# Sums of gathered rows moved from TensorE to GpSimd, gathers spread evenly, and the selection's beats redrawn

## The reference, cut to what matters

```python
scores, idx = top_k(sim, 16)                       # two sides of 64 sub-keys, 8 heads
score = scores[0][..., :, None] + scores[1][..., None, :]
final_scores, pk_idx = top_k(score, 16)            # 16 of 4096 rows for every token and head
w = softmax(final_scores)
k = einsum('bnhk,bnhkd->bnhd', w, keys_table[ind])
v = einsum('bnhk,bnhkd->bnhd', w, values_table[ind])
```

## Time and profile before

| | |
|---|---|
| median of 3 runs | 13968.45 us (13955.31 to 13971.13) |
| the profiled execution | 13932.0 us, span 13929.9 us |
| TensorE (PE) busy | 12687.6 us, 91% |
| VectorE (DVE) busy | 10456.8 us, 75% |
| ScalarE (ACT) busy | 10198.2 us, 73% |
| GpSimd (POOL) busy | 5190.5 us, 37% |
| mean granted TensorE clock | 0.983 of full speed |

### The profile page before, as it was taken

How to read it: one execution, slowest core, us unless ns; L and a number is a source line. 1 busy time by engine, 2 the same in 40 slices (tenths; PEclk the granted TensorE clock), 3 DMA queues, 4 the chain that set the end, 5 groups by cost and what they waited for, 6 DMA issues and landing times.

```text
span 13929.9 us, 337634 instructions
## 1 busy us (share of the span) xinstructions
PE 12687.6 (91%) x87840; PEld 9681.5 (70%) x87840; DVE 10456.8 (75%) x37953; ACT 10198.2 (73%) x24147; POOL 5190.5 (37%) x4136
## 2 busy tenths in 40 slices
PE   6999999999999999999999999999999999999998
PEld 4776766767677667676676766767767677676776
DVE  7777777777777777777777777778777777777774
ACT  5777777777777777777777777777777777777776
POOL 3333333333333333333333333333333333333342
PEclk9999999999999999999999999999999999999998
DMA  2222222222222222222222222222222222222222
GB/s 72 81 79 80 83 79 82 79 81 81 80 80 81 82 81 79 80 84 78 81 81 80 83 79 78 82 81 82 79 80 83 79 81 81 81 81 79 80 84 60
DMA packets 612306, 1112.58 MB, mean 80 GB/s; under 512 B 134096, under 2 KB 150992, under 8 KB 610384
## 3 DMA queue, kind: packets, MB, share of 16 engines
q1 hardware_dynamic: 461648, 816.40, 19.6%
q0 software_dynamic: 131072, 268.70, 7.7%
q10 hardware_dynamic: 17696, 4.46, 0.1%
HBM read 1084.90 MB, written 4.19 MB: 78 GB/s over the span
## 4 chain that ended last, share of the span: by engine, by line
PE 54%; DVE 19%; ACT 11%; DVEq 8%; issue 7%; ACTq 0%; POOL 0%; POOLq 0%
PE p_d L1409 20%; PE p_g L1450 6%; PE p_s L1397 5%; PE p_s L1398 5%; ACT ew L1132 5%; DVE ew L907 5%; PE p_g L1360 3%; DVEq L645 3%; ACT prob L1221 2%; DVE rank_hot L888 2%; PE p_f L1344 2%; PE p_x L1562 2%; PE p_x L1499 2%; ACT gath L1175 1%; PE p_x L1555 1%
## 5 line engine op out<-in xcount | busy, mean ns | idle before, releaser
L1132 ACT ACTIVATE ew<-p_s 128x512 f32<-128x512 f32 x12288 | 7128.0, 611 | 2777.5 <-PE p_s L1398 2550.0
L627 POOL DMA_INDIRECT gath<-in_table,idx x4096 | 5166.5, 1261 | 8585.0 <-PE p_s L1398 8148.6
L1409 PE MATMUL p_d<-ew,tab 128*128 128x256 f32 x24576 | 7621.2, 392 | 494.0 <-DVE ew L907 324.5
L907 DVE SCALAR_TENSOR_TENSOR ew<-ew 128x1024 f32<-128x1024 f32 x3072 | 3753.8, 1222 | 2617.6 <-ACT ew L1132 2516.6
L1409 PEld LDWEIGHTS p_d<-ew,tab 128*128 128x128 f32 x24576 | 3753.3, 193 | 961.7 <-issue 788.0
L1397 PE MATMUL p_s<-mov,rank_sel 128*128 128x256 f16 x12288 | 3380.8, 275 | 200.5 <-ACT ew L1132 131.1
L1398 PE MATMUL p_s<-mov,piece_sel 128*128 128x256 f16 x12288 | 3376.9, 275 | 0.0
L1398 PEld LDWEIGHTS p_s<-mov,piece_sel 128*128 128x128 f16 x12288 | 1211.4, 99 | 1260.7 <-issue 56.0
L1397 PEld LDWEIGHTS p_s<-mov,rank_sel 128*128 128x128 f16 x12288 | 1225.5, 100 | 861.3 <-issue 540.9
L1175 ACT ACTIVATE gath<-gath,kv_w 128x128 f32<-128x128 f32 x4096 | 1445.4, 415 | 0.0
L888 DVE TENSOR_TENSOR rank_hot<-iota_k,rank_key 128x2048 f16<-128x2048 f16 x768 | 933.5, 1216 | 81.5 <-issue 67.5
(11 more groups left out here) (235 smaller groups left out, 11938.0 us busy)
## 6 DMA issues: line engine op xcount, KB each, us to landing
tab<-in_dense_t SPq DMA_DIRECT2D x3072, 256.0 KB
gath<-in_table,idx POOLq DMA_INDIRECT x4096
xin<-in_x SPq DMA_DIRECT2D x64, 128.0 KB
out<-h_out ACTq DMA_DIRECT2D x64, 64.0 KB, 2.2
row_consts<-in_rows SPq DMA_DIRECT2D x1, 548.0 KB, 4.4
w_sb<-in_w SPq DMA_DIRECT2D x1, 512.0 KB, 5.7
w_sb<-in_w ACTq DMA_DIRECT2D x1, 256.0 KB, 4.7
gath<-in_wqpk_t SPq DMA_DIRECT2D x1, 256.0 KB, 5.3
```

Source lines behind the costliest of these rows:

```text
L627: G.indirect_dma_start(out=gath[:, slot, k, :], out_offset=None, in_=table[:, :], in_offset=bass.IndirectOffsetOnAxis(ap=idx[pair.par][:, ...
L907: V.scalar_tensor_tensor(four[:, :, 2 * T:4 * T], four[:, :, 0:2 * T], CHOSEN, four[:, :, 2 * T:4 * T], ALU.is_gt, ALU.mult).then_inc(dens ...
L1132: A.activation(ew[:, c % EW_RING, :], p_s[c % PS_RING][:, :], ACT.Exp).then_inc(dense_e_ready, 1)
L1409: last = M(p_d[:, 0:2 * T], tab[:, u % TAB_RING, i, :], ew[:, c % EW_RING, 2 * T:4 * T], start=(k == 0), stop=(k == CHUNKS - 1))
```

## The change

- TensorE's sums (L1450) and ScalarE's `keep` are gone. GpSimd adds a head's 16 rows up in four steps of `tensor_tensor` (8, 4, 2 and 1 rows of 128), in place and the last into `kv`. Steps wait for each other (`halved`). All four heads are done in a row, due at beats 164.5, 172, 179.5 and 187, on GpSimd's queue ahead of and between the next pair's gathers; `k_tr` now waits for the fourth (`summed`).
- A pair's 64 gathers are due every 2.56 beats, from beat -20.5 to 141. Before, they came in runs of 16 over 38 beats from -45, -4, 51 and 92. `weigh` is due at beats 25.5 to 55, 66.5 to 96, 107.5 to 137 and 148.5 to 178, where it was 2 to 43, 43 to 84, 98 to 139 and 139 to 180.
- The selection's units end at beat 82.8 instead of 92.7, and its rest ends at 164 instead of 159. `front` begins at 65.6 instead of 73.
- The preparation of the first dense head comes 2 to 5 beats later (FIRST_FILL_AT).
- `rank_key` is written by ScalarE in four copies, after the last reader of the old one (`ranks_ready`); VectorE waits for `keys_ready`. `l1_x` is made by ScalarE in 8 activations of 128x128.

```diff
@@ -90,14 +90,17 @@
 SELECT_AT = 6
-SELECT_END = CHUNKS * (DENSE - 1) - 1
+UNITS_END = SELECT_AT + 0.4 * BEATS
+SELECT_END = CHUNKS * (DENSE - 1) + 4
 SELECT_US = 66.0
-    return SELECT_AT + (SELECT_END - SELECT_AT) * us / SELECT_US
+    if us < 4 * UNIT_US:
+        return SELECT_AT + (UNITS_END - SELECT_AT) * us / (4 * UNIT_US)
+    return UNITS_END + (SELECT_END - UNITS_END) * (us - 4 * UNIT_US) / (SELECT_US - 4 * UNIT_US)
@@ -118,6 +121,13 @@
 FILL_AT = (0.25, 6.25, 8.25)
+FIRST_FILL_AT = (5.25, 8.25, 10.25)
+def at_fill(d, part):
+    return at_prep(d, (FILL_AT if d > 0 else FIRST_FILL_AT)[part])
@@ -127,11 +137,9 @@
-def at_sum(j, part):
-    return CHUNKS * ((j + 1) * DENSE // GATHERED - 1) + 22 + part
-WEIGH = min(0.95 * BEATS / (2 * GATHERED), (at_sum(0, 0) - 4) / 2) / (3 - RING // 2)
+SUMS_AT = SELECT_END + 0.5
+GATHER_AT = SUMS_AT + 7 - BEATS
+GATHER_STEP = (BEATS - 28) / (2 * GATHERED * TOPK)
@@ -141,12 +149,17 @@
-    return at_sum(m // 2, 0) - 2 - WEIGH * (2 - m % 2 - part / 4)
+    return at_gather(m + 1, 0) + 5 + 0.72 * TOPK * GATHER_STEP * part / 4
-    return at_weigh(m, 0) - WEIGH * (1 - k / TOPK) - 6
+    return GATHER_AT + GATHER_STEP * (TOPK * m + k)
+def at_add(m):
+    return SUMS_AT + 7.5 * m
@@ -157,10 +170,8 @@
-BANK_ORDER = [k for _, k in sorted([(at_sum(j, 0), ("sum", j)) for j in range(GATHERED)]
-                                   + [(after_dense(d)[1] % BEATS, ("dense", d)) for d in range(DENSE)]
-                                   + [(at_prep(d, FILL_AT[i]), ("map", 3 * d + i))
+BANK_ORDER = [k for _, k in sorted([(after_dense(d)[1] % BEATS, ("dense", d)) for d in range(DENSE)]
+                                   + [(at_fill(d, i), ("map", 3 * d + i))
                                       for d in range(DENSE) for i in range(3)])]
...
@@ -614,11 +627,14 @@
                 if h == 0:
+                    yield at_gather(m, 0) - 0.2
                     hold(pool, idx_ready, 2 * pair.n + p + 1)
-                if m % 2 == 0 and positive(GATHERED * pair.n + m // 2 - 1):
-                    hold(pool, summed, GATHERED * pair.n + m // 2 - 1)
+                if positive(2 * GATHERED * pair.n + m - RING + 1):
+                    yield at_gather(m, 0) - 0.1
+                    hold(pool, summed, 2 * GATHERED * pair.n + m - RING + 1)
                 slot = (2 * GATHERED * pair.par + m) % RING
                 for k in range(TOPK):
+                    yield at_gather(m, k)
                     at = TOPK * h + k
@@ -629,11 +645,36 @@
-        gather(Pair(0, 0, 0))
+        def add_up(pair, m):
+            p, h = divmod(m, GATHERED)
+            slot = (2 * GATHERED * pair.par + m) % RING
+            head = 2 * GATHERED * pair.n + m
+            hold(pool, scaled, head + 1)
+            for i, half in enumerate((8, 4, 2)):
+                if i > 0:
+                    hold(pool, halved, 3 * head + i)
+                G.tensor_tensor(gath[:, slot, 0:half, :], gath[:, slot, 0:half, :], gath[:, slot, half:2 * half, :],
+                                ALU.add).then_inc(halved, 1)
+            hold(pool, halved, 3 * head + 3)
+            G.tensor_tensor(kv[pair.par][:, p, :, h, :], gath[:, slot, 0, :].rearrange("t (s c) -> t s c", s=2),
+                            gath[:, slot, 1, :].rearrange("t (s c) -> t s c", s=2), ALU.add).then_inc(summed, 1)
+        def sums(pair):
+            for m in range(2 * GATHERED):
+                yield at_add(m) - BEATS
+                beat = BEATS * pair.n + int(at_add(m))
+                hold(pool, pair_mm, beat)
+                add_up(pair, m)
+        interleave(gather(Pair(0, 0, 0)))
         with pool.Fori(0, PAIRS // 2 - 1) as it:
             for q in range(2):
-                gather(Pair(2 * it + q + 1, it + q, 1 - q))
-        gather(Pair(PAIRS - 1, (PAIRS - 1) // 2, 1))
+                own = Pair(2 * it + q + 1, it + q, 1 - q)
+                interleave(sums(Pair(2 * it + q, it, q)), gather(own))
+        last = Pair(PAIRS - 1, (PAIRS - 1) // 2, 1)
+        interleave(sums(Pair(PAIRS - 2, (PAIRS - 2) // 2, 0)), gather(last))
+        interleave(sums(last))
@@ -870,18 +911,14 @@
                                 rank_inv[:, None, :, None].to_broadcast([T, 2 * DENSE, TOPK, 2]), ALU.mult)
-            for p in range(2):
-                for s in range(SIDES):
-                    V.tensor_copy(rank_key[:, DENSE * p:DENSE * p + DENSE, :, s, :],
-                                  top_i[:, s, HEADS * p + GATHERED:HEADS * p + HEADS, :, None]
-                                  .to_broadcast([T, DENSE, TOPK, 2]))
-            V_sync()
+            V_sync()
+            dve.wait_ge(keys_ready, count)
             yield from prepare(pair, 0)
             for p in range(2):
-                yield at_prep(d, 2 * p - 9)
+                yield at_fill(d, 0) + 2 * p - 9.2
                 if p == 0 and positive(3 * DENSE * pair.n + 3 * d - 2):
@@ -891,7 +928,7 @@
             for p in range(2):
-                yield at_prep(d, p - 5)
+                yield at_fill(d, 0) + p - 5.2
                 V.tensor_tensor(hots[p][:, :, 0, :, :], hots[p][:, :, 0, :, :],
@@ -965,12 +1002,6 @@
                                    ALU.mult).then_inc(l1_a_ready, 1)
-            yield BACK["l1_x"]
-            dve.wait_ge(l1_o_mm, count)
-            shape = [128, L1_HEADS, L1_HEADS, T // L1_HEADS]
-            V.tensor_tensor(l1_x, px[:, 0, 0:128].rearrange("d (m j) -> d j m", j=L1_HEADS)[:, :, None, :]
-                            .to_broadcast(shape),
-                            head_of[:, None, :, None].to_broadcast(shape), ALU.mult).then_inc(l1_x_ready, 1)
             yield BACK["z"]
@@ -1114,11 +1145,21 @@
+            yield max(at_select(52.0), at_fill(DENSE - 1, 0) - 3)
+            if positive(2 * DENSE * pair.n):
+                act.wait_ge(ranks_ready, 2 * DENSE * pair.n)
+            for p in range(2):
+                for s in range(SIDES):
+                    last = A.copy(rank_key[:, DENSE * p:DENSE * p + DENSE, :, s, :],
+                                  top_i[:, s, HEADS * p + GATHERED:HEADS * p + HEADS, :, None]
+                                  .to_broadcast([T, DENSE, TOPK, 2]))
+            last.then_inc(keys_ready, 1)
             yield from prepare(pair, 0)
             for part, (first, last) in enumerate(FILLS):
-                yield at_prep(d, FILL_AT[part] + (2.15 if part == 0 else 1.15))
+                yield at_fill(d, part) + (2.15 if part == 0 else 1.15)
                 act.wait_ge(map_tr, 3 * DENSE * pair.n + 3 * d + part + 1)
@@ -1178,25 +1219,9 @@
             for kind, k in BANK_ORDER:
-                if kind == "sum":
-                    yield at_sum(k, 5)
-                    keep(pair, k)
-                elif kind == "dense" and k < DENSE - 1:
+                if kind == "dense" and k < DENSE - 1:
                     yield after_dense(k)[1] + 1.15
-        def keep(pair, j):
-            act.wait_ge(summed, GATHERED * pair.n + j + 1)
-            first, second = divmod(2 * j, GATHERED), divmod(2 * j + 1, GATHERED)
-            if first[0] == second[0]:
-                p, h = first
-                last = A.copy(kv[pair.par][:, p, :, h:h + 2, :].rearrange("t s h c -> t h s c"),
-                              p_g[:, 0:256].rearrange("t (h s c) -> t h s c", h=2, s=2))
-            else:
-                for i, (p, h) in enumerate((first, second)):
-                    last = A.copy(kv[pair.par][:, p, :, h, :],
-                                  p_g[:, 128 * i:128 * i + 128].rearrange("t (s c) -> t s c", s=2))
-            last.then_inc(bank_free, 1)
@@ -1246,6 +1271,12 @@
             A.copy(ek[:, :], px[:, 1, 0:128]).then_inc(ek_ready, 1)
+            yield BACK["l1_x"]
+            act.wait_ge(l1_o_mm, count)
+            for h in range(L1_HEADS):
+                last = A.activation(l1_x[:, :, h, :], px[:, 0, 0:128].rearrange("d (m j) -> d j m", j=L1_HEADS),
+                                    ACT.Copy, scale=head_of[:, h:h + 1])
+            last.then_inc(l1_x_ready, 1)
             yield BACK["root2"]
...
@@ -1438,18 +1469,6 @@
                     cross(pair, k)
-                if kind != "sum":
-                    continue
-                for part in range(4):
-                    yield at_sum(k, part)
-                    if part == 0:
-                        hold(pe, bank_free, bank_use(pair, "sum", k))
-                        hold(pe, scaled, 2 * GATHERED * pair.n + 2 * k + 2)
-                    slot = 2 * ((GATHERED * pair.par + k) % 2)
-                    for t in range(4 * part, 4 * part + 4):
-                        last = M(p_g[:, 0:2 * KV], ident[:, :], gath[:, slot:slot + 2, t, :],
-                                 start=(t == 0), stop=(t == TOPK - 1))
-                last.then_inc(summed, 1)
@@ -1465,6 +1484,7 @@
             hold(pe, bank_free, bank_use(pair, "dense", DENSE - 1) + 1)
+            hold(pe, summed, 2 * GATHERED * count)
             hold(pe, q_ready, count)
```

8 lines of the change are left out of this document (5 added, 3 removed).

## The result

The changed kernel takes 13937.13 us (median of 13 runs, 13920.18 to 13953.61) where the one before takes 13966.76: a ratio of 0.998 (95% interval 0.9972 to 0.9988). That is 0.2% faster. The forecast was 13245 us with a range of 13000 to 13700, so the time lies outside it.

What follows compares the result with a forecast made beforehand. TensorE's queue was taken to bound most of the period, VectorE close behind in the second half. Gains of 19.4 us less 8.1 given back leave 11.3 us a pair, times 64 723 us: 13245 us, range 13000 to 13700.

Steps and rivals of the forecast that it cites:

- the one on `rank_key`: ScalarE's key copies at beat 134: 1.3 us at most, wait may hold exponents for a beat, cost 0.
- 13.8 for the sums on TensorE: Beats 80 to 96 and 176 to 192: removing 8 groups of 1.73 us gains 13.8 us a pair.
- 2.2 at `cross`: Around beat 172: TensorE's wait for a map copy goes with the later first fill, gaining 2.2 us a pair.
- 0.9 at the gram: First layer's gram: half of TensorE's 1.8 us wait for VectorE's `xh` goes, gaining 0.9 us a pair.
- 2.5 for masks: Stretches VectorE fills: half of TensorE's 5.1 us wait for masks goes, gaining 2.5 us a pair.
- 1.0 for `l1_x`: Beat 117: 3.0 us of activations on ScalarE, with exponents queued behind, add 1.0 us to the period.
- 5 to 6 us a head on GpSimd: GpSimd's four adds take 5 to 6 us a head; `k_tr` is on time under 9 us.
- rival 4: Slower: a head's sum takes over 9 us and `k_tr` holds TensorE's queue; up to 14397 us, chance 0.08.
- 1.5 for GpSimd holding VectorE: Beats 160 to 192: GpSimd's sums make VectorE pay, costing 1.5 us of period.
- Rival 1: Beats 160 to 192: GpSimd's sums hold VectorE, masks come late, 5 to 6 us more; 13616 us, chance 0.2.
- 5.4 that comes back: Two sum stretches lose their catch-up pause, 1.6 us each, plus 2.2 for stretches behind and denser units: 5.4 us.
- Rival 3: No gain: TensorE's sums only filled time others needed, so the wait moves; 13968 us, chance 0.05.

Runs made afterwards that it cites:

- experiments 1 and 2: Changed kernel with ScalarE's key copy 6 beats later or on VectorE; then either copy place with one add a head or sums on TensorE: 13279.83 to 13839.1 us.
- g: Changed kernel with `rank_key` written by VectorE again, as before the change: 13789.7 us, 0.9873 of the kernel before.
- a: Changed kernel with ScalarE's four `rank_key` copies due 6 beats later: 13323.65 us, 0.9561 of the kernel before.
- l: Changed kernel with the key copy 6 beats later and `l1_x` on VectorE as before: 13492.12 us, 0.9661 of the kernel before.
- f: Changed kernel with the key copy 6 beats later and only the last of each head's four adds: 13279.83 us, 0.9533 of the kernel before.
- experiment 3: Changed kernel with three GpSimd memsets in place of each head's first three adds: 13377.33 us, 0.9596 of the kernel before.
- m: Changed kernel with the key copy 6 beats later and the selection laid out as before the change: 13887.63 us, 0.9942 of the kernel before.
- c: Changed kernel with the sums back on TensorE, at beats 102 and 182: 13839.1 us, 0.993 of the kernel before.
- j: Changed kernel with the key copy 6 beats later and the sums back on TensorE at beats 102 and 182: 13812.27 us, 0.9908.
- n: Changed kernel with the key copy 6 beats later and the hop `kmax` given 7 beats instead of 3: 13371.77 us, 0.9573.
- v: Kernel n with the fourth head's adds alone due 3 beats later: 13386.68 us, 0.9582 of the kernel before.
- u: Changed kernel with the fourth head's adds alone due 3 beats earlier: 14005.55 us, 1.0027 of the kernel before.

## Why the prediction was wrong

The step that failed is the one on `rank_key`: its wait for `ranks_ready` "can hold exponents for a beat; VectorE sets that stretch anyway: 0". The beat was read from the due times. In the queue the last reader had 5 us of VectorE's work ahead of it, the copy waited 4.65 us, and with the four adds behind it that costs 9.7 us a pair (experiments 1 and 2): 3.7 at its own place, the rest downstream. With the copy later the change takes 13323.65 us, inside the 13100 to 13420 given for the forecast by itself. That VectorE set the stretch didn't cover it, because VectorE's masks need those very exponents: both stood still. Two things qualify it. The copies on VectorE, also without the wait, get back only 2.3 us (g), so it is where the copy stands that is worth 9.7, and not the wait alone. And that a lands in the forecast's own range is in part luck, since the terms below missed in both directions.

- **13.8 for the sums on TensorE**: as a gain too large. 7.8 with the key copy late, against sums at 102 and 182. The price of a group was right where TensorE was full (80 to 96 gave 7.4 where 6.7 were expected), but the same four groups at 102 cost a third of that, and at 182 the gain was 3.7 to 4.0 of 6.9.
- **2.2 at `cross`**: held in kind, 137.5 to 28.9 us, 1.7 a pair. **0.9 at the gram**: wrong sign in the changed kernel, 144.7 to 168.3; in a it fell to 32.5, but the next hop (L1363) waits 122.1 for `xh` instead of 6.2. **2.5 for masks**: 324.5 to 202.0, 1.9 a pair, but only while TensorE is held elsewhere: in a it is 349.5, so the gain wasn't there.
- **0.2 for `weigh` in 80 to 96**: the stretch takes 12.3 us and not 13.1. **1.0 for `l1_x`**: 2.1 (l).
- **5 to 6 us a head on GpSimd**: 6.3, inside the bounds, and `k_tr` never waited for GpSimd, so rival 4 was rightly far off.
- **1.5 for GpSimd holding VectorE**: of the right size or too large when nothing else is late (four adds against one 0.6 us, f to a), but 7.5 behind the key wait. Rival 1's mechanism is there, masks up to 4071 ns against 1297, and experiment 3 speaks for the reading of SBUF as what does it: the memsets left the masks alone. Its price depends on what stands beside it, which a single term couldn't say. The Trainium skill (SBUF — State Buffer, "Who interferes with whom") states what the memsets show: only a GpSimd instruction that reads SBUF contends with VectorE's two-input ones.
- **5.4 that comes back**: it can't be told apart from the above. The hops that lost their slack (`kmax`, `xh`) did show as waits: 3.8 us a pair at `neg_kmax` where there were 2.0, and 1.9 at the second `xh` in a where there was 0.1.
- The new beats of the selection were treated as small corrections; by m they are worth 9.0 us a pair, more than the sums.
- Rival 3 gave nearly the right time, 13968, by another way: it had TensorE's sums fill time that others needed. That is so for part of them (c, j); the rest went to a wait that the change added.

Of what was to be seen: 80 to 96 near 14 us (12.3), 176 to 192 near 16 (19.2), and TensorE's busy time of 175 of 203 us, "about as full as before". The last is a slip of the prediction: its own rows add up to 199.5 us of TensorE in the pair, less 13.8 is 185.7, which is 91% of 203.8 where 175 of 203 is 86%. The changed kernel has 190.9, a 187.6.

- **The granted clock**, "no change": at the lower level for 21.3 us of a pair where it was 6.4, and 13.1 in a. How much of the loss is the clock's own, and how much only follows from the waits, no run separates.

What stays open is the hold-up, 2.3 to some 4 us a pair: it shows in the changed kernel, g, l, m, n and v, goes when the fourth head's adds come earlier, are fewer or become memsets, and is absent in a though they are as late there. TensorE signals late in it, and the trace names no cause. One thing goes with it: the traces of these six kernels and of u hold 153428 to 160419 semaphore events, those of the other 13 hold 198795 to 201057. So that the recording of the events has a part in it can't be ruled out.

## What to carry to other kernels

A wait put into a strictly ordered queue costs what stands behind it, and how long it lasts is to be read from the releaser's own queue, from the instructions ahead of it, not from its due time; "the other engine is the bound there" covers nothing when that engine lives on what is held up. Work taken off an engine is worth its length only in stretches that this engine fills. When several edits go together, make the one that adds a wait a run of its own: here one line moved by 6 beats was 9.7 us of 215, and the same work given back to VectorE only 2.3.

## What the runs showed of the hardware

- A GpSimd add of two SBUF inputs can hold VectorE's two-input instructions until it ends, even one of 2 elements: 0.16 us became 2.87 beside a 1024-element add of 2.35, and masks of 1.22 up to 4.07. Beside memsets of 1.6 us no mask took over 1.43. It goes the other way too: the gathers' issue, 0.94 us, took up to 4.02 (2.56 in the kernel before), and the adds of 512, 256 and 128 elements, 1.26, 0.72 and 0.45 us at their shortest, were 1.72, 1.30 and 0.89 on average.
- An add of 1024 elements a partition in float32 takes 2.37 us, 2.3 ns an element, twice the one-input rate worked out from the earlier trace rows. The Trainium skill (GPSIMD Engine Reference, 3.1) gives 4497 ns for 2048, 2.2 ns an element, which the trace bears out; by it the four steps were an estimated 4.2 us where the trace has 6.3. The four at their shortest add up to 4.8 us (2.34 + 1.26 + 0.72 + 0.45); the rest is the drawing out.
- The granted clock, 0.88, 1.00 and 0.97 on average in beats 104 to 112, 136 to 144 and 160 to 168 of the kernel before, was 0.76, 0.85 and 0.76 in the changed one. TensorE waits in each of these stretches or just ahead of it. With the sums on TensorE at 102 the first was 1.00, and with the adds reduced to one or turned into memsets the last was.
